# GNN two-layer kernel: rows' small operations on ScalarE, stage 1's TensorE loop written out, stage 4 with kept adjacency and statistics a chunk further ahead

## What is computed

```python
# layer 0 (8 heads of 32)
n = layernorm(x); q, k, v = n@Wq+bq, n@Wk+bk, n@Wv+bv
w = softmax(q@k.T/sqrt(32) + 2*adj - 1) * (0.25 + 0.75*adj)
x = x + (w / w.sum(-1)) @ v @ Wo + bo
x = x + gelu(layernorm(x)@Wf1+bf1) @ Wf2 + bf2
# layer 1, graph attention, first with 8 heads, then with 1
h = layernorm(x) @ W
s, t = h@a_src, h@a_dst                       # one number per node and head
e = leaky_relu(s[:, None] + t[None, :], 0.2) + adj
x = x + softmax(e) @ h
```

## Time and profile before

| what | value |
|---|---|
| median of 3 runs | 1277.54 us (1277.46 to 1279.42) |
| the profiled execution's own time | 1278.78 us |
| its span in the trace | 1277.0 us |
| instructions | 40299 |
| PE busy | 1169.7 us (92%) |
| PEld busy | 988.7 us (77%) |
| DVE busy | 903.0 us (71%) |
| ACT busy | 643.0 us (50%) |
| POOL busy | 423.7 us (33%) |
| granted TensorE clock, mean | 0.962 |

### The profile page before, as it was taken

One profiled execution on the slowest core, in us unless ns is written; L12 is line 12 of the kernel. 1 busy time (PEld: TensorE's weight loads), 2 busy tenths in 40 slices (PEclk: granted clock), 3 DMA queues, 4 the chain that ended last, 5 costly groups with the idle time before them and its releaser, 6 DMA issues.

```text
span 1277.0 us, 40299 instructions
## 1 busy us (share of the span) xinstructions
PE 1169.7 (92%) x15340; PEld 988.7 (77%) x15340; DVE 903.0 (71%) x2466; ACT 643.0 (50%) x1495; POOL 423.7 (33%) x641
## 2 busy tenths in 40 slices
PE   6699999999999899999999999988888887899998
PEld 5588888878888788989989989866566665677776
DVE  6667766667677745455355454589999999789997
ACT  1576767666676655355354453433333333255554
POOL 2522111211121013123123122055666556644442
PEclk9799999999999999999999999998988989699999
DMA  7010101110000000000000000000000000012232
GB/s 215 23 47 28 52 28 27 28 52 27 28 18 11 3 1 1 1 0 0 0 0 0 0 0 1 9 19 18 15 10 16 16 16 19 11 50 74 81 92 75
DMA packets 50192, 35.50 MB, mean 28 GB/s; under 512 B 5536, under 2 KB 49824, under 8 KB 50080
## 3 DMA queue, kind: packets, MB, share of 16 engines
q1 hardware_dynamic: 45184, 33.04, 8.7%
q10 hardware_dynamic: 4896, 0.80, 0.5%
HBM read 25.44 MB, written 8.39 MB: 26 GB/s over the span
## 4 chain that ended last, share of the span: by engine, by line
PE 63%; DVE 19%; issue 9%; ACT 4%; POOL 3%; DVEq 1%; DMA 1%; ACTq 0%; POOLq 0%; SPq 0%
DVE pp L584 7%; PE BK L1177 5%; PE BK L1262 5%; PE BK L1260 5%; PE BK L1261 5%; PE BK L1053 5%; PE BK L1055 5%; PE BK L1054 5%; PE BK L1151 4%; PE BK L1163 4%; PE F L1078 3%; PE F L1053 2%; PE F L1055 2%; PE F L1054 2%; PE BK L1144 2%
## 5 line engine op out<-in xcount | busy, mean ns | idle before, releaser
L794 POOL TENSOR_TENSOR ve<-mv,eps_l 128x4 f32<-128x4 f32 x64 | 12.9, 202 | 512.4 <-DVE mv L268 512.4
L983 ACT ACTIVATE gf<-BK,bcol 128x512 f32<-128x512 f32 x128 | 88.1, 688 | 187.8 <-PE BK L1055 175.1
L902 ACT ACTIVATE e_sb<-BK,nmx 128x128 f32<-128x128 f32 x512 | 141.4, 402 | 28.5 <-DVE nmx L398 28.5
L1260 PE MATMUL BK<-wf_hi,gh 128*128 128x256 f32 x512 | 145.4, 284 | 0.0
L1262 PE MATMUL BK<-wf_lo,gh 128*128 128x256 f32 x512 | 144.2, 282 | 0.0
L1261 PE MATMUL BK<-wf_hi,gl 128*128 128x256 f32 x512 | 144.0, 281 | 0.0
L584 DVE SCALAR_TENSOR_TENSOR pp<-BK,bqs,gt 128x128 f32<-128x128 f32 x512 | 139.2, 337 | 3.0 <-PE BK L1332 1.3
L491 DVE TENSOR_TENSOR gl<-gf,gh 128x512 fp32r<-128x512 f32 x128 | 92.1, 720 | 67.4 <-ACT gh L984 65.3
L404 DVE TENSOR_TENSOR pt_sb<-BK,ft 128x512 f32<-128x512 f32 x128 | 85.4, 687 | 72.2 <-PE BK L1151 70.6
L505 DVE TENSOR_TENSOR x_all<-BK,x_all 128x256 f32 (+1 forms) x64 | 27.2, 425 | 125.5 <-PE BK L1262 125.5
L263 DVE BATCH_NORM_STATS2 st<-x_all 128x6 f32 (+1 forms) x256 | 96.2, 415 | 10.2 <-DMA x_all<-in_x_dram 8.0
(11 more groups left out here) (180 smaller groups left out, 3067.7 us busy)
## 6 DMA issues: line engine op xcount, KB each, us to landing
adj_in<-in_adj_dram SPq DMA_DIRECT2D x48, 256.0 KB, 3.0
x_all<-in_x_dram SPq DMA_DIRECT2D x16, 512.0 KB, 4.5
out_dram<-y SPq DMA_DIRECT2D x16, 512.0 KB, 3.2
s_wf<-in_L_gnn_Wf_dram SPq DMA_DIRECT2D x2, 1024.0 KB, 12.0
s_w<-in_L_gnn_W_dram SPq DMA_DIRECT2D x2, 256.0 KB, 8.0
s_wq<-in_L_gnn_Wq_dram SPq DMA_DIRECT2D x1, 256.0 KB, 3.6
s_wk<-in_L_gnn_Wk_dram SPq DMA_DIRECT2D x1, 256.0 KB, 4.3
s_wv<-in_L_gnn_Wv_dram SPq DMA_DIRECT2D x1, 256.0 KB, 4.9
```

The costliest lines, as they stand in the source:

```text
L902: e = act.activation(e_sb[:, j, :], LE[:, r, q, :], ACT.Exp, bias=nmx[:, j:j + 1], scale=1.0)
L1260: pe.matmul(dst, gh[:, f, n], hi[:, f, :], start=(f == 0), stop=False)
```

## The change

Six things are done:

1. TensorE's stage 1 is written out, 16 chunks one behind the other, in place of 2 + a loop of 6 x 2 + 2. The other engines keep their loops.
2. Rows, stages 3 and 4: the sign and the 0.8 that `tms` and `u_sb` were multiplied by are put into the weights `wst` and a vector `msc` at setup. The two writes of `tms` move from VectorE to ScalarE (`rows_shift`); `u_sb` becomes four operations, one for each graph, 40 x 128, add and clip in one, straight from PSUM. `bq_out` moves from VectorE to ScalarE. `hb_out` takes two graphs in one operation.
3. `gt_all` keeps the exponential of all 64 adjacencies from stage 3 on, where stage 2's weights lay. Stage 4 no longer loads, transposes or exponentiates them: 16 DMAs, 64 transposes and 16 activations fewer.
4. `d_bcast` spreads from `rp` in rounded format, with rows 32 to 39, as stage 3 does, in place of a float32 product with `rb`. ScalarE makes `rp` in stage 4 too, and GpSimd does `rows_lo` there.
5. Stage 4's statistics are taken two chunks ahead, not one; VectorE's order in a chunk is new, and its share of `normalise` (graph 3) goes to ScalarE, which does graphs 0 and 1 before the rows and 2 and 3 behind them.
6. The first chunk of stage 4 no longer waits for the last chunk of stage 3 before its statistics.

The core of the diff:

```diff
-                    for at, side in ((0, 0), (8, 1), (16, 1), (32, 0), (TROW, 1), (TROW + 8, 1), (TROW + 16, 1)):
-                        done(dve.tensor_copy(wst[:, layer, :, at:at + H], wag[:, layer, side]))
+                    for at, side, factor in ((0, 0, 0.8), (8, 1, 1.0), (16, 1, -0.8), (32, 0, 0.8),
+                                             (TROW, 1, 1.0), (TROW + 8, 1, 1.0), (TROW + 16, 1, 1.0)):
+                        done(dve.tensor_scalar(wst[:, layer, :, at:at + H], wag[:, layer, side], factor, None, ALU.mult))
                     for at in (0, 32):
...
             def rows_max(e):
                 dve.wait_ge(c_st_done, e + 1)
                 dve.tensor_reduce(tmx[:], F[1][TROW:TROW + 24, :].rearrange("p (g n) -> p g n", n=P), AX, ALU.max).then_inc(c_rows, 1)
-                dve.wait_ge(c_rows, e * 5 + 1)
-                dve.tensor_scalar(tms[0:24, :], tmx[:], sgn[0:24, 0:1], None, ALU.mult).then_inc(c_rows, 1)
-                dve.tensor_copy(tms[32:40, :], tmx[0:8, :]).then_inc(c_rows, 1)
 
             def rows_exponent(e, layer):
-                dve.wait_ge(c_rows, e * 5 + 3)
-                dve.scalar_tensor_tensor(out=u_sb[:].rearrange("p (g n) -> p g n", n=P),
-                                         in0=F[1][0:ROWS, :].rearrange("p (g n) -> p g n", n=P), scalar=cb[layer][:, 0:1],
-                                         in1=tms[:].unsqueeze(2).to_broadcast([ROWS, G, P]), op0=ALU.add, op1=ALU.add).then_inc(c_rows, 1)
-                dve.wait_ge(c_rows, e * 5 + 4)
-                dve.tensor_scalar(u_sb[:], u_sb[:], scl[:, 0:1], EXP_LIMIT, ALU.mult, ALU.min).then_inc(c_rows, 1)
-
-            def hb_view(par, layer):
-                if layer == 0:
-                    return hb[par][:, 0:G * H * HA].rearrange("p (g h c) -> p g h c", g=G, h=H)
-                return hb[par][:, 0:G * (D + 1)].rearrange("p (g h c) -> p g h c", g=G, h=1)
-
-            def bq_out(e, par, layer):
-                heads = (H, 1)[layer]
-                dve.wait_ge(c_bqt, e + 1)
-                dve.tensor_copy(bq_sb[par][:], F[1][:].rearrange("p (g c) -> p g c", c=P)[:, :, 0:24]).then_inc(c_bq, 1)
-                dve.wait_ge(c_bq, e + 1)
-                dve.tensor_copy(hb_view(par, layer)[:, :, :, D // heads], bq_sb[par][:, :, 8:8 + heads]).then_inc(c_one, 1)
+                dve.wait_ge(c_tms, e + 1)
+                for g in range(G):
+                    r = dve.tensor_scalar(u_sb[:, g * P:(g + 1) * P], F[1][0:ROWS, g * P:(g + 1) * P], tms[:, g:g + 1], EXP_LIMIT,
+                                          ALU.add, ALU.min)
+                r.then_inc(c_rows, 1)
 
             def hb_out(e, par, n):
                 dve.wait_ge(c_h, e * 2 + n + 1)
-                for g in range(2 * n, 2 * n + 2):
-                    r = dve.tensor_tensor(hb_view(par, 0)[:, g, :, 0:HD],
-                                          F[n][:, (g % 2) * D:(g % 2 + 1) * D].rearrange("p (h d) -> p h d", h=H),
-                                          bq_sb[par][:, g, 8:8 + H].unsqueeze(2).to_broadcast([P, H, HD]), ALU.mult)
-                r.then_inc(c_hb, 1)
+                dve.tensor_tensor(hb_view(par, 0)[:, 2 * n:2 * n + 2, :, 0:HD],
+                                  F[n][:].rearrange("p (g h d) -> p g h d", g=2, h=H),
+                                  bq_sb[par][:, 2 * n:2 * n + 2, 8:8 + H].unsqueeze(3).to_broadcast([P, 2, H, HD]),
+                                  ALU.mult).then_inc(c_hb, 1)
 
             def next_stats(i, graphs):
...
 
             def c2_step(i, half, par):
                 back = not (isinstance(i, int) and i == 0)
-                more = not (isinstance(i, int) and i == NC - 1)
+                early = not (isinstance(i, int) and i >= NC - 2)
+                prev = (i - 1, half - (1 - par), 1 - par)
                 ln_lo(i + CD)
                 if back:
                     d_scale(i - 1, 1 - par)
-
-                if more:
-                    for g in range(2 if back else 0, G):
-                        if not back and g == 0:
-                            dve.wait_ge(c_x, C_START + NG)
-                        stats(i + CD + 1, i + 1, g)
-                rows_max_and_aggr(i, CD)
-                rows_exponent(i + NC, 1)
-                for g in range(3):
-                    if back:
-                        d_recip(i - 1, g)
-                prev = (i - 1, half - (1 - par), 1 - par)
-                if more:
-                    normalise(i + CD + 1, i + 1, (3,))
-                if back:
-                    d_norm(*prev, 0)
-                early = not (isinstance(i, int) and i >= NC - 2)
+                rows_max(i + NC)
                 if early:
                     stats(i + CD + 2, i + 2, 0)
-                bq_out(i + NC, par, 1)
+                    stats(i + CD + 2, i + 2, 1)
+                rows_exponent(i + NC, 1)
                 if back:
-                    d_norm(*prev, 1)
-                    d_norm(*prev, 2)
+                    for g in range(3):
+                        d_recip(i - 1, g)
+                    for g in range(3):
+                        d_norm(*prev, g)
+                if early:
+                    stats(i + CD + 2, i + 2, 2)
+                    stats(i + CD + 2, i + 2, 3)
+                    dve.wait_ge(ln_nm, nm_count(i + CD + 1, CD))
+                    dve.wait_ge(ln_st, (i + CD + 3) * G)
+                if back:
                     d_recip(i - 1, 3)
+                if early:
+                    aggr(i + CD + 2)
+                if back:
                     d_norm(*prev, 3)
-                if early:
-                    stats(i + CD + 2, i + 2, 1)
+            dve.wait_ge(c_x, C_START + 2 * G)
+            for g in range(G):
+                stats(CD + 1, 1, g)
+            dve.wait_ge(ln_nm, nm_count(CD, CD))
+            dve.wait_ge(ln_st, (CD + 2) * G)
+            aggr(CD + 1)
             chunks(dve, c2_step)
             d_scale(NC - 1, 1)
             for g in range(G):
...
                     if first == CC:
                         rows_lo(i, par)
                         add_bias(i, CC, c1_bc, c_xb)
+                    if first == CD:
+                        add_bias(i, CD, c2_bc, d_xb)
+                        pool.wait_ge(d_xb, (i + 1) * G)
+                        rows_lo(i + NC, par)
                 def rows_lo(e, par):
                     pool.wait_ge(c_rp, e + 1)
                     pool.tensor_tensor(rp[par][32:40, :], rb[32:40, :], rp[par][32:40, :].bitcast(F32), ALU.subtract).then_inc(c_lo, 1)
...
                 c = i + first
                 if not (isinstance(c, int) and c == CC):
                     ln_hi(c)
-                if first == CD and not (isinstance(i, int) and i == 0):
-                    d_hb(i - 1, 1 - par, 1)
-                act.wait_ge(adj_t, c - NC + 1)
-                act.activation(gt_sb[par][:].rearrange("p g n -> p (g n)"), F[0][:], ACT.Exp).then_inc(c_gt, 1)
                 if first == CC:
-                    act.wait_ge(c_rows, i * 5 + 5)
+                    act.wait_ge(adj_t, c - NC + 1)
+                    act.activation(gt_all[:, bass.ds(i * W4, W4)], F[0][:], ACT.Exp).then_inc(c_gt, 1)
+                    rows_shift(i, 0)
+                    act.wait_ge(c_rows, i * 2 + 2)
                     wait_for(act, c_lo, i)
                     act.activation(rb[0:ROWS, :], u_sb[:], ACT.Exp).then_inc(c_rb, 1)
                     act.activation(rp[par][0:ROWS, :], u_sb[:], ACT.Exp).then_inc(c_rp, 1)
+                    bq_out(i, par, 0)
                     normalise(i, CC, range(G))
                 else:
-                    act.wait_ge(c_rows, (i + NC) * 5 + 5)
-
-                    if isinstance(i, int) and i == 0:
-                        act.wait_ge(c_lo, NC)
-                    else:
-                        act.wait_ge(d_bc, i)
+                    if not (isinstance(i, int) and i == 0):
+                        d_hb(i - 1, 1 - par, 1)
+                    normalise(i, CD, (0, 1))
+                    rows_shift(i + NC, 1)
+                    act.wait_ge(c_rows, (i + NC) * 2 + 2)
+                    act.wait_ge(c_lo, i + NC)
                     act.activation(rb[0:ROWS, :], u_sb[:], ACT.Exp).then_inc(c_rb, 1)
-                    normalise(i, CD, (0, 1, 2))
+                    wait_for(act, d_bc, i - 1)
+                    act.activation(rp[par][0:ROWS, :], u_sb[:], ACT.Exp).then_inc(c_rp, 1)
+                    bq_out(i + NC, par, 1)
+                    normalise(i, CD, (2, 3))
+
+            def rows_shift(e, layer):
+
+                act.wait_ge(c_rows, e * 2 + 1)
+                act.activation(tms[0:24, :], tmx[:], ACT.Identity, bias=cb[layer][0:24, 0:1], scale=msc[0:24, 0:1])
+                act.activation(tms[32:40, :], tmx[0:8, :], ACT.Identity, bias=cb[layer][0:8, 0:1],
+                               scale=msc[0:8, 0:1]).then_inc(c_tms, 1)
+
+            def bq_out(e, par, layer):
+                heads = (H, 1)[layer]
```

(35 more changed lines are left out.)

24 lines of the change are left out of this document (13 added, 11 removed).

## The result

| | before | after |
|---|---|---|
| time, median | 1277.59 us (4 runs) | 1226.55 us (1226.13 to 1227.21, 4 runs) |
| ratio | | 0.9598, 95% interval 0.9581 to 0.9614 |
| profiled execution: span, time | 1277.0, 1278.78 us | 1224.5, 1226.81 us |

The account below looks back on a forecast made before the run. It took TensorE to bound stages 1 and 2, VectorE stage 3, and a dependency ring stage 4. Savings 15.4 + 40.9 + 1 + 1 = 58.3 us from 1278.8 gave 1220.5, forecast as a 1219 us median, range 1209 to 1238.

Parts of the forecast that it names:

- Stage 1: TensorE written out: twelve looped chunks at 23.93 to 24.08 us in place of 25.28, saving 15.4 us, lower end 0.
- rival 3: Stage 1: the straight code does not run straight and gains nothing, 1234 us; chance 0.06.
- Stage 3's mechanism: Stage 3: VectorE loses 2.17 us a chunk and stays the bound, chunks 14.3 us for 17.22, saving 40.9 us.
- little room left: Stage 3: TensorE's own work is at most 14.0 us a chunk, close under VectorE's 14.3.
- The half clock of stage 3: Stage 3: TensorE's waits for `pp` and `rb` lower its clock, costing 0.73 us a chunk, 10.2 in all; shrinking them ends this.
- VectorE's own sum: Stage 3 before the change: VectorE's operations through one chunk, without idle time between them, take 16.49 us.
- Rival 2: Stage 3 gains only VectorE's sum, or TensorE becomes the bound: 1230 to 1235 us; chance 0.15.
- The two small terms of 1 us: First chunks of stages 3 and 4: a shorter row chain, and no wait for the last residuals, 1 us saved each.
- The change leaves its loop as it is: Stage 2: TensorE alone bounds it and its loop is unchanged, so only stages 1, 3 and 4 can move.
- its ring: Stage 4: a dependency cycle from transposes through `xl`, `wst`, `c_b_turn` and `xn`, 9.8 us a chunk for 9.82, no gain.
- rivals 1 and 4: Stage 4's half clock from idle TensorE: in every second chunk, 1232 us, chance 0.17; throughout, slower, up to 1291, chance 0.03.
- Rival 5: ScalarE's `tms` is late in every chunk and VectorE stands, 1 to 2 us a chunk, 1245 us; chance 0.04.

## Why the prediction was right, and where it was off

It put 58.3 us together; the profiled execution gave 52.0. By its steps:

- **Stage 1, right.** 15.4 forecast, 14.7 in the chunks it named (24.06 each for 24.0); alone it gave 15.1, undone 11.3, where the loop ran without the low clock. Straight code didn't pay what the loop's turn pays (rival 3 falls).
- **Stage 3's mechanism, right; its size 3.7 us too large** (14.56 for 14.3, 14 times). Of this 1.5 us are `u_sb`: I took 0.92 between 0.80 and 1.04, and it is 1.03, the upper end, where the Trainium skill (VectorE: DVE Perf Modes, the section on the TRN2 errata) had put it; `pp` at the same width from PSUM, at 0.259, was the right row to go by. Another 2.8 are the gap ahead of head 0 (0.23 us at 898.17), 0.16 to 0.24 in every chunk, where TensorE has just become the later one, as "little room left" said. Against that, 1.5 came back that weren't in the sum: behind `tmx` the next operation now starts 0.62 us after it (890.74 before 891.36) in place of 0.73 (910.48 before 911.21). The last 0.9 I can't place.
- **The half clock of stage 3, right**: 0.92 to 1.00, and back at 0.89 with `tms` on VectorE. But the reason that I gave for it is only half shown: the wait for `pp` did go, from 1.56 us a chunk to 0.16, that for `rb` kept 11.2 of 13.1, and the clock was full all the same. The 16.49 of VectorE's own sum was right too: chunks of the kernel before at full clock are that long. Rival 2 falls.
- **Chunk 15 of stage 3 was left out of the sum**, though its VectorE work is that of the others: 4.2 us more than forecast, together with the way into stage 4.
- **The two small terms of 1 us failed.** The stretch to stage 3's chunk 1 took 24.55 for 24.56. Stage 4's chunk 0 took 13.11 for 12.99: the rows' new `tms` is queued on ScalarE behind `xn`, which waits until 1063.84 for GpSimd, and only then starts at 1064.84. The text named that queue and took a gain all the same. With `tms` on VectorE the chunk took 12.35, which bears it out.
- **"The change leaves its loop as it is" was the step that failed outright.** Stage 2's code didn't change, its addresses did: 3.0 us slower. Nothing in the profile before could have shown it, but the diff shows a tile of 512 bytes gone from in front of the others.
- **Stage 4, right by its ring, and to the hundredth (9.80) by luck.** TensorE waits 1.34 us for `xl`, `xn` ends the wait before the transposes, and the kept adjacency was worth nothing. But two terms were off and cancelled: from the `wst` products to `c_b_turn` it is 5.09 us for 4.9, since `rb` comes only 0.2 us sooner and still holds TensorE up by 0.12, and `c_b_turn` with what stands between it and `xn` is 0.89 for 1.06. The half clock of rivals 1 and 4 didn't come in its chunks (1.00 in the window), though TensorE idles 1.34 us in each; in the kernel with stage 1's loop it did reach chunk 1. Rival 5 falls as well.

Together the pieces make what the sum of 58.3 had over the 52.5 of the spans: 1.6 in stage 1 (0.7 in its chunks, 0.9 around them), 3.7, 1.0, 1.1 and 3.0, less 4.2 and less 0.5 in stage 4's chunks. Those between stages are no surer than 2 us, since they differ by that between kernels with the same code there.
